# Reordering two ScalarE steps of the K/V phase and adding 72 matmuls to the first attention tile of a transformer layer on eight cores

## Chip, cores and metric

The kernel runs on the 8 cores of one Trainium2 chip. Every core works on two of the 16 sequences and exchanges nothing with the others. The metric is the device time of the slowest core in microseconds.

## What is computed

One post-norm transformer layer: linear attention (elu + 1 as feature map, 16 heads of 64), then an FFN with SiLU gate and integer weights, each with a residual and a layer norm.

```python
q = elu(x @ Wq.T) + 1; k = elu(x @ Wk.T) + 1; v = x @ Wv.T       # x: (16, 2048, 1024)
KV = einsum('bshd,bshe->bhde', k, v); k_sum = k.sum(axis=1)
out = einsum('bshd,bhde->bshe', q, KV) / (einsum('bshd,bhd->bsh', q, k_sum) + 1e-6)
x = layernorm(x + out @ Wo.T)
h = silu(x @ (w_gate/127).T) * (x @ (w_up/127).T)                # hidden 3072
x = layernorm(x + h @ (w_down/127).T)
```

## The kernel before

Each core takes its two sequences of 2048 tokens in turn. The order of instructions on each engine is the order in which the program text issues them; semaphores tie the engines together, and every DMA is issued on SyncE's one queue (SP).

**Phase 1** (`phase1`, once for a sequence) computes K, V and the sum of k^T v over 16 chunks of 128 tokens. Numbers u of chunks count from 0. For a chunk:
- PE: 16 matmuls of K (L552) into one pair of PSUM banks (`kps`), 16 of V (L568) into the other (`vps`). The pairs swap roles with each chunk: K of chunk u+1 writes the banks that held V of chunk u, and V of chunk u+1 those that held K of u. Then come 16 small matmuls k^T v of the chunk before (L486, `emit_kv`).
- DVE adds these into `kv_acc` (L504), takes min(K, 0) into `t1` (L585), and later writes `k_tm` = max(K, 0) + exp (L604).
- ACT takes the exponential `texp` of `t1` (L590) and copies V from PSUM to `v_tm` (L596). Ahead of them in a chunk it casts the next chunk's x to bf16 (L450). SP loads x two chunks ahead (L441) and transposes the cast x into `xT` (L459).

In the first sequence the same loop also converts weights (`drain_w_jobs`, four jobs a chunk): wq and wo in chunks 0 to 3, with a load, an ACT cast (L385) and a store each; w_down in chunks 4 to 9, with a load (L344) and a cast on DVE or GpSimd (L353) into `wd_buf`; then wk and wv are stored from `wpair` (L330). After phase 1 `load_pair` puts wq and wo where wk and wv were (L426).

**Phase 2** (`phase2`, once for a tile of 512 tokens, four to a sequence) computes Q (L816, 64 matmuls), multiplies by the summed KV in eight steps of 4 matmuls (L864, `emit_c1h`), each followed on DVE by three steps that free its banks, transposes the result by DMA (L925), projects it by wo (L941, `emit_c2`) and normalises (`ln_chunk`). Between these steps `pend_half` puts the down projection of the previous tile (L735, 48 matmuls for 128 tokens). In the very first tile there is no previous one: `pend` is None, and the first four calls of `pend_half` issue the loads of the first gate and up weights instead (`fill_jobs`, L1042), the last two nothing. `pre_pend` is true in the first tile of each sequence, `skip_a` in every tile.

**Phase 3** (`phase3`) computes gate (L1135) and up (L1148) in 24 blocks and h (L1167 on ACT, L1175 on DVE).

PE's matmuls in the places above are 128x512, except L864 (128x130) and L486 (128x65). The two operations that the change swaps, in their order before:

```python
t_exp = P.op("scalar", lambda e: e.activation(texp[:], t1[:], AF.Exp), waits=[t_min, ...])
t_v = P.op("scalar", lambda e: e.activation(v_tm[:, kr, :, 0:HD], vps[:]..., AF.Copy), waits=brd(vbk) + ...)
```

Of the kernel before, what the change touches and what calls it, by code (L numbers as in the profile page):

```python
# [10 lines left out]
AF = mybir.ActivationFunctionType  # L11
# [171 lines left out]
def build_program(n_seq=NSEQ, n_tiles=NTILE // NSEQ, stop_after=None):  # L183
# [17 lines left out]
    with contextlib.ExitStack() as ctx:  # L201
        E = ctx.enter_context
        wpair = E(nc.sbuf_tensor("wpair", [128, 2, NJ, D], BF16))
        wd_buf = E(nc.sbuf_tensor("wd_buf", [128, NM, D], BF16))
# [14 lines left out]
        t1 = E(nc.sbuf_tensor("t1", [128, D], BF16))  # L219
        texp = E(nc.sbuf_tensor("texp", [128, D], BF16))  # L220
# [10 lines left out]
        P = Prog(nc, ctx)  # L231
# [3 lines left out]
        def bw(keys):  # L235
            return [BK[k].begin_write() for k in keys]
# [4 lines left out]
        def bend(keys, tok):  # L241
            for k in keys:
                BK[k].end_write(tok)
# [8 lines left out]
        d_view = ps_c[:].rearrange("p (r e) -> p r e", r=2)  # L252
# [12 lines left out]
        tr_t1 = Track()  # L265
        tr_texp = Track()
# [9 lines left out]
        tr_wd = [Track() for _ in range(NM)]  # L276
# [8 lines left out]
        tok = P.op("vector", lambda v: v.memset(consts[:, 0:1], EPS_LN))  # L285
        tr_consts.add_write(tok)
        tok = P.op("vector", lambda v: v.memset(consts[:, 1:2], -0.5))
        tr_consts.add_write(tok)
        tok = P.op("vector", lambda v: v.memset(consts[:, 2:3], INV127))
        tr_consts.add_write(tok)  # L290
        for r in range(2):
            tok = P.op("vector", lambda v, r=r: v.memset(v_tm[:, r, :, HD:HD + 1], 1.0))
# [180 lines left out]
        def phase1(s, first, pre_x=False):  # L473
            NCH = SEQ // 128
            pend = {}
# [58 lines left out]
            for u in range(NCH):  # L534
                p1_cast(u + 1)
                tq = order[u] % CPT
                kr = u % 2
                kvr = u % 2
                if first:
                    drain_w_jobs(4)  # L540

                kps = ps_a if u % 2 == 0 else ps_b
                vps = ps_b if u % 2 == 0 else ps_a
                kbk = ("a0", "a1") if u % 2 == 0 else ("b0", "b1")
                vbk = ("b0", "b1") if u % 2 == 0 else ("a0", "a1")
                for j in range(NJ):
                    for hl in range(2):
                        last = (j == NJ - 1 and hl == 1)
                        tok = P.op(
                            "tensor",  # L550
                            lambda t, j=j, hl=hl, tq=tq, kps=kps:
                            t.matmul(kps[:, hl * 512:(hl + 1) * 512],  # L552
                                     xT[:, j, tq * 128:(tq + 1) * 128],
                                     wpair[:, 0, j, hl * 512:(hl + 1) * 512],
                                     start=(j == 0), stop=(j == NJ - 1)),
                            waits=[tr_xT[tq].reads(), tr_wp[0][j].reads()]
                                  + (bw(kbk) if (j == 0 and hl == 0) else []),
                            inc=last)
                bend(kbk, tok)
                p1_ld(u + 2)  # L560
                p1_tp(u + 1)
                for j in range(NJ):
                    for hl in range(2):
                        last = (j == NJ - 1 and hl == 1)
                        tok = P.op(
                            "tensor",
                            lambda t, j=j, hl=hl, tq=tq, vps=vps:
                            t.matmul(vps[:, hl * 512:(hl + 1) * 512],  # L568
                                     xT[:, j, tq * 128:(tq + 1) * 128],
                                     wpair[:, 1, j, hl * 512:(hl + 1) * 512],  # L570
                                     start=(j == 0), stop=(j == NJ - 1)),
                            waits=[tr_xT[tq].reads(), tr_wp[1][j].reads()]
                                  + (bw(vbk) if (j == 0 and hl == 0) else []),
                            inc=last)
                bend(vbk, tok)
                tr_xT[tq].add_reader(tok)
                for j in range(NJ):
                    tr_wp[0][j].add_reader(tok)
                    tr_wp[1][j].add_reader(tok)

                if u > 0:
                    emit_kv(u - 1)

                t_min = P.op("vector",
                             lambda v, kps=kps: v.tensor_scalar_min(t1[:], kps[:], 0.0),  # L585
                             waits=brd(kbk) + [tr_t1.begin_write()])
                bread(kbk, t_min)
                tr_t1.end_write(t_min)
                t_exp = P.op("scalar",
                             lambda e: e.activation(texp[:], t1[:], AF.Exp),  # L590
                             waits=[t_min, tr_texp.begin_write()])
                tr_t1.add_reader(t_exp)
                tr_texp.end_write(t_exp)
                t_v = P.op("scalar",
                           lambda e, kr=kr, vps=vps:
                           e.activation(v_tm[:, kr, :, 0:HD],  # L596
                                        vps[:].rearrange("p (h e) -> p h e", h=H),
                                        AF.Copy),
                           waits=brd(vbk) + [tr_vtm[kr].begin_write()])
                bread(vbk, t_v)  # L600
                tr_vtm[kr].add_write(t_v)
                t_k = P.op("vector",
                           lambda v, kr=kr, kps=kps:
                           v.scalar_tensor_tensor(k_tm[:, kr, :], kps[:], 0.0,  # L604
                                                  texp[:], ALU.max, ALU.add),
                           waits=[t_exp] + brd(kbk)
                                 + [tr_ktm[kr].begin_write()])
                bread(kbk, t_k)
                tr_texp.add_reader(t_k)
                tr_ktm[kr].end_write(t_k)  # L610
                pend[u] = (kr, kvr, t_k, t_v)

            emit_kv(NCH - 1)
            if first:
# [4 lines left out]
                      waits=[tr_kvbd.begin_write()])  # L619
            c0 = P.op("vector",  # L620
                      lambda v: v.tensor_copy(kvbd[0:64, :, 0:HD + 1],
                                              kv_acc[0:64, :, :]),
                      waits=[z0, tr_kvacc.reads()])
# [3 lines left out]
                      waits=[z0, tr_kvacc.reads()])  # L627
# [99 lines left out]
        def down_half(sc, hl):  # L727
            pr = sc % 2
            bank = ("c0", "c1", "c2", "c3")[pr * 2 + hl]
            for hm in range(NM):  # L730
                last = (hm == NM - 1)
                tok = P.op(
                    "tensor",
                    lambda t, hm=hm, hl=hl, sc=sc, pr=pr:
                    t.matmul(d_view[:, pr, hl * 512:(hl + 1) * 512],  # L735
                             h_fm[:, hm, sc * 128:(sc + 1) * 128],
                             wd_buf[:, hm, hl * 512:(hl + 1) * 512],
                             start=(hm == 0), stop=(hm == NM - 1)),
                    waits=[tr_h[hm].reads(), tr_wd[hm].reads()]
                          + (bw((bank,)) if hm == 0 else []),  # L740
                    inc=last)
            bend((bank,), tok)
            for hm in range(NM):
                tr_h[hm].add_reader(tok)
                tr_wd[hm].add_reader(tok)
            down_toks[(sc, hl)] = tok
# [33 lines left out]
        def phase2(s, g, stop2=None, skip_a=False, pend=None, slot3=3,  # L780
# [6 lines left out]
            def px(step):  # L787
# [13 lines left out]
                elif step == 5:  # L801
                    load_x_fin(nxt[2], 2)
                    load_x_fin(nxt[3], 3)

            if pre_pend and pend is not None:
                down_half(0, 0)
                down_half(0, 1)
            q_toks = {}
            for i in range(NJ):
                abk = "a0" if i % 2 == 0 else "a1"  # L810
                for j in range(NJ):
                    last = (j == NJ - 1)
                    tok = P.op(
                        "tensor",
                        lambda t, i=i, j=j:
                        t.matmul(ps_a[:, (i % 2) * 512:(i % 2 + 1) * 512],  # L816
                                 wpair[:, 0, j, i * 128:(i + 1) * 128],
                                 xT[:, j, :], start=(j == 0), stop=(j == NJ - 1)),
                        waits=[tt.reads() for tt in tr_xT] + [tr_wp[0][j].reads()]
                              + (bw((abk,)) if j == 0 else []),  # L820
                        inc=last)
# [3 lines left out]
                for tt in tr_xT:  # L825
                    tt.add_reader(tok)
                t_min = P.op("vector",
                             lambda v, i=i:
# [13 lines left out]
                           lambda v, i=i:  # L842
# [135 lines left out]
            def pend_half(sc, hl):  # L978
                if pend is not None:
                    down_half(sc, hl)  # L980
                elif fill_jobs:
                    fill_jobs.pop(0)()

            def pend_fin(sc):
                if pend is not None:
# [303 lines left out]
```

How the kernel before makes its waits and increments, by code:

```python
        def closure(eng, fn=fn, real_waits=real_waits, tok=tok, sem=sem):  # L128
            for s, v in real_waits:
                eng.wait_ge(s, v)
            inst = fn(eng)
            if tok is not None:
                inst.then_inc(sem, 1)
# [15 lines left out]
        def closure(e, fn=fn, real_waits=real_waits, sem=sem):  # L149
            for s, v in real_waits:
                e.wait_ge(s, v)
            fn(e).then_inc(sem, 16)
# [7 lines left out]
        def closure(eng, real_waits=real_waits):  # L160
            for s, v in real_waits:
                eng.wait_ge(s, v)
```

## Time and profile before

| what | us |
|---|---|
| median of the two timed runs | 1977.47 |
| the two timed runs | 1959.79 and 1995.15 |
| the profiled execution | 1951.59 |
| its span, first to last instruction of core 1 | 1950.1 |
| phase 1 of the first sequence, first K matmul to last kv matmul | 19 to 267 |
| the first tile's Q to its first gate matmul | 270 to 354 |
| phase 1 of the second sequence | 991 to 1205 |

The profile is of the slowest core of one execution. The span leaves out what lies before the first and behind the last instruction. Engines: PE is the matmul engine, DVE the vector engine, ACT the scalar engine, SPq the queue on which SyncE issues DMAs. In a row of the timeline the first number is the start, the second the time that the row covers; in brackets stands how long the engine was idle ahead of it and what ended that.

### The profile page before, as it was taken

What the parts mean: (1) busy time and instruction counts of PE and PEld (TensorE: products, weight loads), DVE (VectorE), ACT (ScalarE), POOL (GpSimd) and SP (SyncE); (2) the same over time, 40 slices, a digit from 0 to 9 for tenths busy, and PEclk for the clock granted to TensorE, in tenths of its full rate; (3) what the DMA queues carried; (4) which work ended last, traced back from release to release, by engine and by line L of the source; (5) the groups of instructions that cost most, each with busy time, mean ns of one, the idle gap of its engine ahead of it and who ended that gap; (6) DMA issues with size and microseconds to landing.
All of it is one profiled execution on the core that took longest, in us unless ns stands there. A gap on an engine that the chain in (4) does not pass through costs nothing.

```text
span 1950.1 us, 23065 instructions; the slowest of 8 cores (1931.0 to 1950.1 us)
## 1 busy us (share of the span) xinstructions
PE 1602.9 (82%) x7424; PEld 697.3 (36%) x7424; DVE 520.4 (27%) x979; ACT 541.8 (28%) x801; POOL 42.3 (2%) x44
## 2 busy tenths in 40 slices
PE   2666664778999899997986677889899989989998
PEld 0222221333444344443432223334344434434443
DVE  1132232123321332332222222421331232133211
ACT  2421211212342252233112221341243225223312
POOL 0010001121000000000000000000000000000000
PEclk9888886899999999998997888989999999999999
DMA  7987227795444145336522222245235515522431
GB/s 221 268 252 251 44 87 205 216 314 194 105 129 155 55 109 168 103 91 195 152 81 65 49 54 92 65 120 154 81 112 141 150 53 131 153 76 62 130 112 44
DMA packets 213236, 255.28 MB, mean 131 GB/s; under 512 B 136320, under 2 KB 136320, under 8 KB 212096
## 3 DMA queue, kind: packets, MB, share of 16 engines
q1 hardware_dynamic: 213120, 253.81, 45.0%
q8 instruction: 64, 1.05, 0.2%
q14 instruction: 52, 0.43, 0.1%
HBM read 184.55 MB, written 37.75 MB: 114 GB/s over the span
## 4 chain that ended last, share of the span: by engine, by line
PE 68%; DMA 10%; DVE 8%; ACT 6%; issue 5%; SPq 1%; POOL 1%; DVEq 0%; ACTq 0%; POOLq 0%
PE ps_c L735 18%; PE ps_a L1135 15%; PE ps_b L1148 15%; PE ps_b L941 5%; PE ps_a L552 4%; PE ps_b L552 4%; PE ps_a L568 2%; PE ps_b L568 2%; DVE t L829 2%; ACT texp L836 2%; DVE t L585 2%; PE ps_a L816 2%; DVE q_fm L843 2%; DMA scr_wu<-wgu 1%; ACT v_tm L596 1%
## 5 line engine op out<-in xcount | busy, mean ns | idle before, releaser
L1135 PE MATMUL ps_a<-ln1T,wgu 128*128 128x512 bf16 x1536 | 369.0, 384 | 26.2 <-DMA ln1T<-ln_bf 9.4
L1148 PE MATMUL ps_b<-ln1T,wgu 128*128 128x512 bf16 x1536 | 368.5, 383 | 19.2 <-DVE h_fm L1175 19.2
L735 PE MATMUL ps_c<-wd_buf,h_fm 128*128 128x512 bf16 x1536 | 354.3, 390 | 0.0
L1167 ACT ACTIVATE silu_b<-ps_a,consts 128x512 bf16<-128x512 f32 x192 | 131.4, 688 | 521.1 <-PE ps_a L1135 461.4
L1175 DVE SCALAR_TENSOR_TENSOR h_fm<-ps_b,silu_b 128x512 bf16<-128x512 f32 x192 | 131.9, 691 | 489.1 <-PE ps_b L1148 454.9
L1135 PEld LDWEIGHTS ps_a<-ln1T,wgu 128*128 128x128 bf16 x1536 | 151.2, 99 | 214.8 <-issue 39.9
L1148 PEld LDWEIGHTS ps_b<-ln1T,wgu 128*128 128x128 bf16 x1536 | 150.6, 99 | 207.2 <-issue 31.9
L735 PEld LDWEIGHTS ps_c<-wd_buf,h_fm 128*128 128x128 bf16 x1536 | 153.2, 101 | 185.7 <-issue 19.3
L552 PE MATMUL ps_a<-wpair,xT 128*128 128x512 bf16 x256 | 88.3, 515 | 98.7 <-ACT v_tm L596 57.7
L941 PE MATMUL ps_b<-wpair,attnT 128*128 128x512 bf16 x512 | 135.0, 424 | 30.5 <-DVE res L965 14.2
L816 PE MATMUL ps_a<-xT,wpair 128*128 128x512 bf16 x512 | 126.8, 398 | 30.9 <-DVE q_fm L843 27.2
L639 ACT ACTIVATE texp<-res 128x1024 bf16<-128x1024 f32 x64 | 67.3, 1051 | 297.3 <-DVE res L758 233.9
L552 PE MATMUL ps_b<-wpair,xT 128*128 128x512 bf16 x256 | 86.0, 511 | 73.3 <-ACT v_tm L596 65.7
L590 ACT ACTIVATE texp<-t 128x1024 bf16<-128x1024 bf16 x32 | 33.7, 1055 | 293.2 <-DVE t L585 292.8
L941 PEld LDWEIGHTS ps_b<-wpair,attnT 128*128 128x128 bf16 x512 | 53.3, 107 | 102.4 <-issue 60.5
L504 DVE TENSOR_TENSOR kv_acc<-kv_acc,ps_c 128x520 f32<-128x520 f32 x30 | 20.9, 697 | 251.9 <-PE ps_c L486 251.9
L816 PEld LDWEIGHTS ps_a<-xT,wpair 128*128 128x128 bf16 x512 | 48.7, 101 | 107.4 <-issue 62.0
L552 PEld LDWEIGHTS ps_a<-wpair,xT 128*128 128x128 bf16 x256 | 29.9, 123 | 150.7 <-issue 140.8
L552 PEld LDWEIGHTS ps_b<-wpair,xT 128*128 128x128 bf16 x256 | 30.8, 125 | 123.1 <-issue 112.9
L836 ACT ACTIVATE texp<-t 128x512 bf16<-128x512 bf16 x64 | 40.3, 629 | 120.4 <-DVE t L829 120.4
L864 PE MATMUL ps_a<-kvbd,q_fm 128*128 128x130 bf16 x256 | 29.4, 238 | 49.4 <-DVE attn_bf L906 30.8
L843 DVE SCALAR_TENSOR_TENSOR q_fm<-ps_a,texp 128x512 bf16<-128x512 f32 x64 | 44.3, 692 | 64.3 <-ACT texp L836 64.3
(61 smaller groups left out, 879.1 us busy)
## 6 DMA issues: line engine op xcount, KB each, us to landing
wgu<-scr_wg SPq DMA_DIRECT2D x168, 256.0 KB, 2.6
wgu<-scr_wu SPq DMA_DIRECT2D x168, 256.0 KB, 2.6
x_f<-x SPq DMA_DIRECT2D x56, 512.0 KB, 4.4
out<-outb SPq DMA_DIRECT2D x32, 512.0 KB, 2.7
outb<-wgi SPq DMA_DIRECT2D x14, 512.0 KB, 6.4
outb<-wui SPq DMA_DIRECT2D x14, 512.0 KB, 7.2
outb<-wdi SPq DMA_DIRECT2D x12, 512.0 KB, 5.0
wgu<-wdi SPq DMA_DIRECT2D x12, 512.0 KB, 6.5
```

The costliest lines, as they stand in the source:

```text
L552: t.matmul(kps[:, hl * 512:(hl + 1) * 512], xT[:, j, tq * 128:(tq + 1) * 128], wpair[:, 0, j, hl * 512:(hl + 1) * 512], start=(j == 0), st ...
L568: t.matmul(vps[:, hl * 512:(hl + 1) * 512], xT[:, j, tq * 128:(tq + 1) * 128], wpair[:, 1, j, hl * 512:(hl + 1) * 512], start=(j == 0), st ...
L639: e.activation(texp[:], res[:, rr, :], AF.Square, accum_out=stats[:, sl, 1:2]),
L735: t.matmul(d_view[:, pr, hl * 512:(hl + 1) * 512], h_fm[:, hm, sc * 128:(sc + 1) * 128], wd_buf[:, hm, hl * 512:(hl + 1) * 512], start=(hm ...
L816: t.matmul(ps_a[:, (i % 2) * 512:(i % 2 + 1) * 512], wpair[:, 0, j, i * 128:(i + 1) * 128], xT[:, j, :], start=(j == 0), stop=(j == NJ - 1)),
L836: lambda e: e.activation(texp[:, 0:TILE], t1[:, 0:TILE], AF.Exp),
L843: v.scalar_tensor_tensor(q_fm[:, i, :], ps_a[:, (i % 2) * 512:(i % 2 + 1) * 512], 0.0, texp[:, 0:TILE], ALU.max, ALU.add),
L941: t.matmul(ps_b[:, hl * 512:(hl + 1) * 512], attnT[:, tc, e_, :], wpair[:, 1, e_, hl * 512:(hl + 1) * 512], start=(e_ == 0), stop=(e_ == N ...
L1135: t.matmul(ps_a[:, (m % 2) * 512:(m % 2 + 1) * 512], wgu[:, 0, r, j * 128:(j + 1) * 128], ln1T[:, j, :], start=(j == 0), stop=(j == NJ - 1)),
L1148: t.matmul(ps_b[:, (m % 2) * 512:(m % 2 + 1) * 512], wgu[:, 1, r, j * 128:(j + 1) * 128], ln1T[:, j, :], start=(j == 0), stop=(j == NJ - 1)),
L1167: e.activation(silu_b[:, m % 2, :], ps_a[:, (m % 2) * 512:(m % 2 + 1) * 512], AF.Silu, scale=consts[:, 2:3]),
L1175: v.scalar_tensor_tensor(h_fm[:, m, :], ps_b[:, (m % 2) * 512:(m % 2 + 1) * 512], INV127, silu_b[:, m % 2, :], ALU.mult, ALU.mult),
```

## The change

Two edits. In phase 1 the ACT copy of V is issued ahead of the exponential, in all 32 chunks. In phase 2 a function `warm_mms(n)` issues n matmuls of 128x512 whose result, in PSUM bank c0, nobody reads (`wd_buf` times `wd_buf`). It is called with 24 ahead of Q, and with 8 in every call of `pend_half` without a pending tile. Both occur in the first tile of the first sequence alone: 24 + 6 x 8 = 72 matmuls. The branch with `not skip_a` is never taken.

```diff
@@ phase1
-                t_exp = P.op("scalar",
-                             lambda e: e.activation(texp[:], t1[:], AF.Exp),
-                             waits=[t_min, tr_texp.begin_write()])
-                tr_t1.add_reader(t_exp)
-                tr_texp.end_write(t_exp)
                 t_v = P.op("scalar",
...
                 tr_vtm[kr].add_write(t_v)
+                t_exp = P.op("scalar",
+                             lambda e: e.activation(texp[:], t1[:], AF.Exp),
+                             waits=[t_min, tr_texp.begin_write()])
+                tr_t1.add_reader(t_exp)
+                tr_texp.end_write(t_exp)
@@ phase2
+            def warm_mms(n):
+                for i in range(n):
+                    last = (i == n - 1)
+                    tok = P.op(
+                        "tensor",
+                        lambda t:
+                        t.matmul(d_view[:, 0, 0:512],
+                                 wd_buf[:, 0, 0:128],
+                                 wd_buf[:, 1, 0:512],
+                                 start=True, stop=True),
+                        waits=[tr_wd[0].reads(), tr_wd[1].reads()]
+                              + (bw(("c0",)) if i == 0 else []),
+                        inc=last)
+                bend(("c0",), tok)
+                tr_wd[0].add_reader(tok)
+                tr_wd[1].add_reader(tok)
+
             if pre_pend and pend is not None:
                 down_half(0, 0)
                 down_half(0, 1)
+            elif pre_pend and pend is None and not skip_a:
+                pass
+            elif pre_pend:
+                warm_mms(24)
@@ pend_half
-                elif fill_jobs:
-                    fill_jobs.pop(0)()
+                else:
+                    if fill_jobs:
+                        fill_jobs.pop(0)()
+                    warm_mms(8)
```

On ACT, in chunk 1 of the first sequence, with its last weight cast ahead and the cast of x of the next chunk behind:

```order
 L385 ACTIVATE h_fm<-res 128x1024 [waits sem_scalar,dsl_wf0,dsl_scw3]
-L590 ACTIVATE texp<-t 128x1024 [waits sem_vector,sem_scalar]
-L596 ACTIVATE v_tm<-ps_a 128x16x64 [waits sem_tensor]
+L591 ACTIVATE v_tm<-ps_a 128x16x64 [waits sem_tensor]
+L598 ACTIVATE texp<-t 128x1024 [waits sem_vector,sem_scalar]
 L450 ACTIVATE x_bf<-x_f 128x1024 [waits dsl_x1]
```

The copy of V, which waits for the matmuls of V alone, now stands ahead of the exponential, which waits for DVE. All else on ACT keeps its place.

On PE, before, from the last kv matmuls of the first sequence over the first tile's attention to phase 3:

```order
L486 MATMUL ps_c<-v_tm,k_tm 64x65 x32
L816 MATMUL ps_a<-xT,wpair 128x512 x64
L864 MATMUL ps_a<-kvbd,q_fm 128x130 x16
L941 MATMUL ps_b<-wpair,attnT 128x512 x16
L864 MATMUL ps_a<-kvbd,q_fm 128x130 x8
L941 MATMUL ps_b<-wpair,attnT 128x512 x16
L864 MATMUL ps_a<-kvbd,q_fm 128x130 x8
L941 MATMUL ps_b<-wpair,attnT 128x512 x32
```

And in the changed kernel, at the start of the same stretch (L811 are the added matmuls, L837 is Q, L885 the product with KV, L962 the projection by wo):

```order
L486 MATMUL ps_c<-v_tm,k_tm 64x65 x32
L811 MATMUL ps_c<-wd_buf 128x512 x24
L837 MATMUL ps_a<-xT,wpair 128x512 x64
L885 MATMUL ps_a<-kvbd,q_fm 128x130 x8
L811 MATMUL ps_c<-wd_buf 128x512 x8
L885 MATMUL ps_a<-kvbd,q_fm 128x130 x4
L811 MATMUL ps_c<-wd_buf 128x512 x8
L885 MATMUL ps_a<-kvbd,q_fm 128x130 x4
L962 MATMUL ps_b<-wpair,attnT 128x512 x16
```

And at its end, where phase 3 begins (L1158):

```order
L885 MATMUL ps_a<-kvbd,q_fm 128x130 x8
L962 MATMUL ps_b<-wpair,attnT 128x512 x32
L811 MATMUL ps_c<-wd_buf 128x512 x16
L1158 MATMUL ps_a<-ln1T,wgu 128x512 x8
```

Added are 24 matmuls ahead of Q, 8 ahead of four of the steps with KV, and 16 behind the last projection. Nothing else moved on PE.

## Rows read from the trace of the kernel before

**Rows 1.** The page's first line, the slowest of eight cores.

```profile
span 1950.1 us, 23065 instructions; the slowest of 8 cores (1931.0 to 1950.1 us)
```

**Rows 2.** K matmuls (L552): idle us until each releaser, times.

```profile
  ACT v_tm L596: 123.4, 28
...
  DMA xT<-x_bf: 12.2, 2
```

**Rows 3.** Timeline of one chunk, sequence 2: start, us, engine, line, instruction.

```profile
1017.92 3.62 PE L568 MATMUL ps_b<-wpair,xT 128*128 128x512 bf16 x16
...
1021.47 0.45 PE L486 MATMUL ps_c<-v_tm,k_tm 128*64 128x65 bf16 x16
1022.09 0.69 DVE L504 TENSOR_TENSOR kv_acc<-kv_acc,ps_c 128x520 f32<-128x520 f32 x1 [10.15 <-PE ps_c L486]
1022.70 1.22 DVE L585 TENSOR_SCALAR t<-ps_a 128x1024 bf16<-128x1024 f32 x1
1024.07 1.06 ACT L590 ACTIVATE texp<-t 128x1024 bf16<-128x1024 bf16 x1 [12.54 <-DVE t L585]
1025.03 1.01 ACT L596 ACTIVATE v_tm<-ps_b 128x1024 bf16<-128x1024 f32 x1
1025.23 1.22 DVE L604 SCALAR_TENSOR_TENSOR k_tm<-ps_a,texp 128x1024 bf16<-128x1024 f32 x1 [1.31 <-ACT texp L590]
1025.93 1.05 ACT L450 ACTIVATE x_bf<-x_f 128x1024 bf16<-128x1024 f32 x1
...
1026.29 5.88 PE L552 MATMUL ps_b<-wpair,xT 128*128 128x512 bf16 x16 [4.38 <-ACT v_tm L596]
```

**Rows 4.** Timeline of PE, phase 1 of the second sequence.

```profile
1000.03 3.61 PE L552 MATMUL ps_b<-wpair,xT 128*128 128x512 bf16 x16 [1.48 <-ACT v_tm L596]
1003.48 3.62 PE L568 MATMUL ps_a<-wpair,xT 128*128 128x512 bf16 x16
...
1190.40 5.74 PE L552 MATMUL ps_b<-wpair,xT 128*128 128x512 bf16 x16 [4.38 <-ACT v_tm L596]
```

**Rows 5.** Timeline of PE, phase 1 of the first sequence.

```profile
102.21 5.30 PE L552 MATMUL ps_a<-wpair,xT 128*128 128x512 bf16 x16 [4.84 <-ACT v_tm L596]
...
115.72 5.30 PE L552 MATMUL ps_b<-wpair,xT 128*128 128x512 bf16 x16 [4.38 <-ACT v_tm L596]
...
169.76 5.77 PE L552 MATMUL ps_b<-wpair,xT 128*128 128x512 bf16 x16 [4.38 <-ACT v_tm L596]
...
197.24 5.30 PE L552 MATMUL ps_b<-wpair,xT 128*128 128x512 bf16 x16 [4.38 <-ACT v_tm L596]
...
252.12 5.30 PE L552 MATMUL ps_b<-wpair,xT 128*128 128x512 bf16 x16 [4.47 <-ACT v_tm L596]
```

**Rows 6.** Windows: stretch, length, busy us of each engine, granted clock, DMA share, GB/s.

```profile
57.22:102.21 44.99, 28.34 (x144) 11.60 (x145) 9.00 (x9) 20.99 (x22) 0.00 (x0) 0.84 0.99 265
115.72:169.76 54.04, 36.52 (x193) 15.29 (x194) 17.88 (x21) 11.66 (x13) 9.81 (x9) 0.85 0.68 218
169.76:197.24 27.48, 18.72 (x96) 7.70 (x97) 7.30 (x9) 5.82 (x7) 0.00 (x0) 0.86 0.81 239
1026.29:1190.40 164.11, 111.53 (x576) 46.16 (x577) 36.67 (x37) 34.70 (x36) 0.00 (x0) 0.83 0.22 52
276.01:289.80 13.79, 11.32 (x49) 4.27 (x49) 8.03 (x13) 3.78 (x6) 0.00 (x0) 1.00 0.00 1
298.72:351.00 52.28, 23.50 (x80) 9.08 (x80) 12.80 (x35) 15.70 (x27) 8.32 (x8) 0.66 0.72 191
```

**Rows 7.** DMA issues: queue, kind, count, median us to landing.

```profile
xT<-x_bf SPq DMA_TRANSPOSE x56, 3.2
```

**Rows 8.** Timeline of PE, end of phase 1 to phase 3, first sequence.

```profile
266.04 0.47 PE L486 MATMUL ps_c<-v_tm,k_tm 128*64 128x65 bf16 x16 [4.79 <-DVE k_tm L604]
...
270.13 5.09 PE L816 MATMUL ps_a<-xT,wpair 128*128 128x512 bf16 x16 [3.62 <-DMA wpair<-scr_wq]
...
315.74 6.16 PE L941 MATMUL ps_b<-wpair,attnT 128*128 128x512 bf16 x16 [5.36 <-DMA attnT<-attn_bf]
...
353.77 3.57 PE L1135 MATMUL ps_a<-ln1T,wgu 128*128 128x512 bf16 x8 [9.37 <-DMA ln1T<-ln_bf]
```

## Prediction

> **What bounds the kernel now.** I read the page first, then the waits of the K matmuls, then one chunk of phase 1 in order of time, and last the windows by stage. The span is 1950.1 us on core 1, and the cores lie within 1% of each other [rows 1]. The one large wait that this change touches is in phase 1, the K and V projections of 32 chunks of 128 tokens: the K matmuls (L552) sat idle for 123.4 us in 28 waits until ACT's copy of V (L596), about 4.4 us each, and for 12.2 us until a transpose of x [rows 2].
>
> One chunk in order of time shows why the wait is that long [rows 3]. V's matmuls start at 1017.92 and end at 1021.54, and the small kv matmuls end at 1021.92. Then a chain runs: DVE adds kv into kv_acc (0.69), DVE takes the minimum of K (1.22), ACT the exponential (1.06), and only then ACT copies V out of ps_b (1.01). V had been complete since 1021.54, but ACT works its queue in order and the exponential stands ahead. PE needs ps_b for the next K and starts at 1026.29, after 4.38 us of idleness. The second half of the price is in that same row: the 16 K matmuls then take 5.88 us, while 16 V matmuls take 3.62. The granted clock over this part of phase 1 is 0.83 [rows 6]: it falls to its lower level, 1.2 GHz, in each stall and comes back to 2.4 GHz in the course of K. A stall of 1.48 us did not do that: the K at 1000.03 took 3.61 us after it and V started 3.45 us after K, which is 0.216 us a matmul [rows 4]. Eight matmuls at the low level took 3.57 us, about 0.43 each [rows 8].
>
> **The swap on ACT, second sequence.** V's copy goes ahead of the exponential. It then waits for V's matmuls alone. The row at 1000.03 shows what that gives: behind the first chunk of the sequence, which has no kv step ahead of its exponential, V's copy alone was missing, and K came after 1.48 us of idleness [rows 4]. So K can start at V's end + 1.48 and, at full clock, end its stream 3.45 later, at + 4.93. The exponential loses nothing: its input is ready 2.4 us after V's end (1023.92 less 1021.54), the copy is over by about 1.2, and k_tm ends as now, at 1025.23 + 1.22 = 1026.45, which is 4.91 behind V's end [rows 3]. That is the wait that is late next: V of the next chunk writes the bank that k_tm reads, so it starts at + 4.91 + 0.2 = + 5.1, and with 3.62 for V itself the period becomes 8.7 us. PE is then idle for about 1.0 us ahead of K and 0.2 ahead of V. The Q stage has a comparable pattern, PE busy 11.32 of 13.79 us in short stalls, with a granted clock of 1.00 [rows 6], so I take the clock as held. The K starts of 1000.03 and 1190.40 are 14 periods apart [rows 4], 13.60 us each. 14 x (13.60 - 8.7) = 68.6 us. The last K goes from 5.74 to 3.62: 2.1 us.
>
> Queued behind the exponential on ACT is the cast of x (L450), and behind it on SP's queue the transpose of x, which lands in 3.2 us at the median [rows 7]. The cast now follows k_tm's input as before, so it ends about 4.8 us behind V's end and the transpose lands at about 8.3; the K that reads it starts at 8.7 + 1.5 = 10.2. That is hidden with 2 us to spare. DMA was busy for 0.22 of this stretch, 3 us a chunk of the 13.6 [rows 6], so it has room here.
>
> **The swap, first sequence.** The same chunks run beside the conversion of the other weights, and the DMA share tells how much can be gained [rows 6].
> - Chunks 1 to 3 (57.22 to 102.21): DMA is at 0.99. ACT also carries four weight casts a chunk ahead of both operations, each waiting for its DMA. I take 1.0 us in all, the copy that no longer stands behind the exponential at the end.
> - Chunk 4 (102.21 to 115.72, 13.51 us [rows 5]): K starts cold, then the short stall. A stream takes 0.17 less than its row says, since the next begins under its end (3.62 and 3.45): 5.13 + 3.45 + 1.48 = 10.1, a gain of 3.4.
> - Chunks 5 to 8 (115.72 to 169.76): share 0.68 of 54.04 is 36.7 us of DMA, 9.2 a chunk, more than 8.7. I take 9.5, since loads, stores and transposes share one queue and don't pack fully: 54.0 - 38.0 = 16.0. Ends: 8.7 (gain 19.2) and no gain at all, if each load group must land before the next is issued.
> - Chunks 9 and 10 (169.76 to 197.24), with the stores of wk and wv, 2 MB each: 0.81 x 27.48 = 22.3 us of DMA is the floor: 5.2. Ends 10.1 and 0.
> - Chunks 11 to 14 (197.24 to 252.12), nothing beside them: 54.88 - 4 x 8.7 = 20.1, and the last K 1.7.
> Sum of the first sequence 47.4, of the second 70.7.
>
> **The 24 matmuls ahead of Q.** They enter after the kv matmuls, which end at 266.04 + 0.47 = 266.5 [rows 8], where PE now waits until 270.13 for wq. The kv matmuls had a 4.79 us stall ahead, so the clock is low: 24 x 0.216 + 1.7 for the ramp (as in K, 5.30 against 3.62 [rows 5, 4]) = 6.9, until 273.4. Q starts 3.3 later than the weights allow but without its own ramp (5.09 against 3.62): net 1.8 us lost. Ends: 0.1 (24 at 0.216) and 5.2 (24 at 0.43).
>
> **The six groups of 8.** They stand between the attention steps of the first tile. Each costs 1.7 us of PE at full clock and 3.4 at the low one. There PE is busy for 23.50 of 52.28 us with DMA at 0.72 [rows 6], and the second projection by wo waited 5.36 us for the DMA of attnT [rows 8]. That transpose stands on SP's queue behind the loads of gate and up weights, which don't hang on PE. Four groups lie where PE waits for DVE or DMA, two (16 matmuls) in the 9.37 us in front of the first gate matmul at 353.77 [rows 8]; they end too early to warm it. I take 0. Ends: 48 x 0.43 = 20.6 lost, or 7.5 gained, if three projections of 16 run as V does (3.62 in place of 6.16).
>
> **A rule weighed.** The rows put the ramp at 29 K groups of about 1.7 us, 49 us or 2.5% of the span. The Trainium skill, page "TensorE: Matmul & The Clock Gate", Part 1, holds that the ramp penalty is under 1% of a typical kernel's span. By that rule the clock could give back at most 19.5 us in place of about 49, and the sum would come out some 30 us smaller. The trace disagrees, since the cold start returns with every chunk.
>
> **The sum.** 47.4 + 70.7 - 1.8 = 116.3 us. The profiled execution took 1951.59 us, 1.5 more than its span, which gives 1835.3. The two timed runs are 8.2 and 43.6 above that execution, their median 25.9; I go by the lower and predict 1843.
>
> **Rivals.**
> 1. The two short stalls together still drop the clock at each K. Then a period is 1.48 + 5.13 + 3.46 = 10.1: 14 x 3.5 = 49 in the second sequence, 38 in the first (1.0 + 3.4 + 13.6 + 5.2 + 14.5), less 1.8: 85, or 1875 us. For it: 4.4 us of stall do it every time. Against: the K behind 1.48 us, and the Q stage.
> 2. SP's one queue binds where weights are converted: chunks 5 to 10 keep their time. The sum loses 21.2: 95 and 1865 us. For it: share 0.68 to 0.81, and K waited for xT twice. Against: the queue is idle for a third of that time.
> 3. The copy was not what PE waited for (the profile names the latest event only), and nothing is gained. Then only the added matmuls count, 2 to 20 us: about 1970. Against: the 28 waits of equal length.
> 4. Slower: phase 1 is split into stalls too short for a pause and too frequent for the clock, which stays at 1.2 GHz through K and V. The period is then 6.9 + 6.9 + 1.5 = 15.3 against 13.6; over 25 chunks 42 us, and 72 added matmuls at 0.43 are 31: up to 73 slower, 2033 us. It decides as soon as V too runs at 0.43. Against: the same rows as in 1; each V behind a slow K took 3.62 us.
>
> **Chances.** The forecast 0.74, rival 1 0.09, rival 2 0.12, rival 3 0.03, rival 4 0.02. The low end takes DMA at its best (8) and the gain in the projections (7.5) with a base at the profiled time: 1835 - 15 = 1820, and 5 for small things: 1815. The high end takes rivals 1 and 2 and 20 us for a base at the median: 1892. A measurement tells 2%, some 39 us, from no change; rivals 1 and 2 are beyond it as well, so faster 0.95, same 0.03, slower 0.02.
>
> **What would show it.** Right: in the second sequence K starts 8.7 us apart, K's 16 matmuls take 3.6, the granted clock there is near 1.00, the idle time of L552 until V's copy is near 1 us a chunk, and a new wait of V (L568) for k_tm appears. The added matmuls stand from about 219 us (266 less 47) for about 7 us, and Q right behind. Wrong: K of 5 us after the short stall (rival 1), K waiting for xT in chunks 5 to 10 (rival 2), K still 4 us behind V (rival 3), V of 6.8 us (rival 4), or more than 89 us from Q's start to the first gate matmul, which are 84 now.

## The result and the profile after

The changed kernel took 1844.88 us in the median of 9 runs (1840.81 to 1852.92). The kernel before, run beside it, took 1952.15 in the median of 8. The ratio is 0.945, with a 95% interval of 0.9428 to 0.9473: 107 us less. Some executions on all eight cores were disturbed, with longer times on the same kernel; the medians and ratios below leave them out, and where that left too few for an interval, the text gives the lowest time. The forecast was 1843 us and faster, so the total fits. It is so close by luck in part: two errors cancel, told below.

The page of the changed kernel, its first line and the engines' busy time, answers to [rows 1]:

```profile
span 1848.0 us, 23214 instructions; the slowest of 8 cores (1826.4 to 1848.0 us)
...
PE 1571.8 (85%) x7496; PEld 690.3 (37%) x7496; DVE 520.2 (28%) x979; ACT 544.9 (29%) x801; POOL 42.6 (2%) x44
```

PE is busy for 31 us less (1602.9 before) although 72 matmuls were added: K's 16 matmuls take 3.61 us in most chunks now, where they took 5.30 and more. The waits of K (L552), against [rows 2]:

```profile
  DMA xT<-x_bf: 28.5, 7
  ACT v_tm L591: 20.8, 20
  ACT texp L598: 15.1, 3
```

Of 123.4 us behind V's copy 20.8 are left, 1.04 each. The wait for transposes of x grew from 12.2 to 28.5 us; a third entry names the exponential, three waits ahead of chunks 3 to 5, of which more below.

One chunk of the second sequence in order of time, which answers to [rows 3]:

```profile
997.04 3.61 PE L568 MATMUL ps_b<-wpair,xT 128*128 128x512 bf16 x16
...
1000.58 0.45 PE L486 MATMUL ps_c<-v_tm,k_tm 128*64 128x65 bf16 x16
1000.75 1.03 ACT L591 ACTIVATE v_tm<-ps_b 128x1024 bf16<-128x1024 f32 x1 [4.24 <-PE ps_b L568]
1001.21 0.70 DVE L504 TENSOR_TENSOR kv_acc<-kv_acc,ps_c 128x520 f32<-128x520 f32 x1 [4.31 <-PE ps_c L486]
1001.82 1.22 DVE L585 TENSOR_SCALAR t<-ps_a 128x1024 bf16<-128x1024 f32 x1
...
1002.03 3.61 PE L552 MATMUL ps_b<-wpair,xT 128*128 128x512 bf16 x16 [1.00 <-ACT v_tm L591]
1003.48 1.06 ACT L598 ACTIVATE texp<-t 128x1024 bf16<-128x1024 bf16 x1 [1.70 <-DVE t L585]
...
1004.64 1.23 DVE L604 SCALAR_TENSOR_TENSOR k_tm<-ps_a,texp 128x1024 bf16<-128x1024 f32 x1 [1.60 <-ACT texp L598]
...
1006.01 3.61 PE L568 MATMUL ps_a<-wpair,xT 128*128 128x512 bf16 x16 [0.37 <-DVE k_tm L604]
```

V's matmuls end at 1000.65, ACT copies V at 1000.75 instead of behind the exponential, and K starts at 1002.03, 1.00 us after PE's last kv matmul. K takes 3.61 us. The new wait is in the last row: V of the next chunk stands until DVE's k_tm step has read its banks. Here it is 0.37 us; in most chunks V starts 3.69 us behind K, where a free stream takes 3.45.

Three windows, the second sequence and chunks 5 to 8 and 9 to 10 of the first, against [rows 6] (columns as there):

```profile
984.71:1089.38 104.67, 91.21 (x577) 39.79 (x578) 36.94 (x37) 36.35 (x36) 0.00 (x0) 1.00 0.40 81
112.57:150.20 37.63, 31.45 (x193) 14.01 (x193) 16.48 (x20) 10.96 (x11) 8.88 (x8) 0.95 1.11 314
150.20:175.56 25.36, 15.20 (x96) 6.62 (x97) 9.55 (x10) 8.11 (x8) 2.30 (x2) 0.86 1.07 331
```

The granted clock of the second sequence went from 0.83 to 1.00. In the first sequence the DMA share passed 1. A share above 1 can only arise where the times of packets overlap, so 1 is not a full engine and no ceiling.

To place the gain I compared the same start times on PE on all eight cores, before and after. Each row is the mean length of a stage over the cores in one execution.

| stage | before | after | forecast change | measured change |
|---|---|---|---|---|
| sequence 1, chunks 1 to 3 | 43.1 | 43.5 | -1.0 | +0.4 |
| chunk 4 | 13.8 | 10.6 | -3.4 | -3.2 |
| chunks 5 to 8 | 54.6 | 37.2 | -16.0 | -17.4 |
| chunks 9 and 10 | 27.2 | 26.8 | -5.2 | -0.4 |
| chunks 11 to 14 | 55.0 | 36.7 | -20.1 | -18.3 |
| last K to the last kv | 14.4 | 13.1 | -1.7 | -1.3 |
| last kv to Q | 3.4 | 6.8 | +3.3 | +3.4 |
| Q to the first gate matmul | 82.2 | 80.2 | -1.5 | -2.0 |
| from there to the second tile's Q | 111.0 | 112.9 | 0 | +1.9 |
| to sequence 2 | 523.1 | 525.2 | 0 | +2.1 |
| phase 1 of sequence 2 | 213.4 | 143.2 | -70.7 | -70.2 |
| the rest | 744.9 | 745.8 | 0 | +0.9 |

### The profile page after: what moved, and what is told of

The parts are those of the page before. It is cut to its first block, busy times and chain, and to the rows that moved or that the text cites. A ratio compares the mean times of both kernels' runs of the same rounds, so it can differ in the third digit from the quotient of the medians.

```text
span 1848.0 us, 23214 instructions; the slowest of 8 cores (1826.4 to 1848.0 us)
## 1 busy us (share of the span) xinstructions
PE 1571.8 (85%) x7496; PEld 690.3 (37%) x7496; DVE 520.2 (28%) x979; ACT 544.9 (29%) x801; POOL 42.6 (2%) x44
## 4 chain that ended last, share of the span: by engine, by line
PE 67%; DMA 12%; DVE 7%; ACT 6%; issue 4%; SPq 2%; POOL 1%; DVEq 0%; ACTq 0%; POOLq 0%
PE ps_c L735 18%; PE ps_a L1158 16%; PE ps_b L1171 15%; PE ps_b L962 5%; PE ps_b L552 3%; PE ps_a L552 3%; PE ps_a L568 3%; DMA outb<-wui 3%; PE ps_b L568 2%; DVE t L850 2%; ACT texp L857 2%; DMA xT<-x_bf 2%; DVE q_fm L864 2%; PE ps_a L837 2%; DMA attnT<-wui 1%
## 5 line engine op out<-in xcount | busy, mean ns | idle before, releaser
L1158 PE MATMUL ps_a<-ln1T,wgu 128*128 128x512 bf16 x1536 | 367.0, 382 | 23.2 <-DMA wgu<-scr_wg 8.6
L1158 PEld LDWEIGHTS ps_a<-ln1T,wgu 128*128 128x128 bf16 x1536 | 150.4, 98 | 209.7 <-issue 33.3
L962 PE MATMUL ps_b<-wpair,attnT 128*128 128x512 bf16 x512 | 131.9, 417 | 33.4 <-DMA attnT<-attn_bf 16.3
L837 PE MATMUL ps_a<-xT,wpair 128*128 128x512 bf16 x512 | 125.3, 394 | 27.4 <-DVE q_fm L864 27.4
L552 PE MATMUL ps_a<-wpair,xT 128*128 128x512 bf16 x256 | 67.0, 415 | 59.2 <-ACT wpair L415 35.4
L552 PE MATMUL ps_b<-wpair,xT 128*128 128x512 bf16 x256 | 63.0, 403 | 40.5 <-DMA xT<-x_bf 19.5
L962 PEld LDWEIGHTS ps_b<-wpair,attnT 128*128 128x128 bf16 x512 | 52.4, 105 | 102.8 <-issue 59.1
L837 PEld LDWEIGHTS ps_a<-xT,wpair 128*128 128x128 bf16 x512 | 48.6, 100 | 102.8 <-issue 56.3
L885 PE MATMUL ps_a<-kvbd,q_fm 128*128 128x130 bf16 x256 | 28.7, 234 | 43.3 <-DVE attn_bf L927 24.8
L758 DVE SCALAR_TENSOR_TENSOR res<-ps_c,ln_bf 128x1024 f32<-128x1024 f32 x32 | 39.0, 1219 | 82.8 <-PE ps_c L735 79.9
L552 PEld LDWEIGHTS ps_a<-wpair,xT 128*128 128x128 bf16 x256 | 24.8, 102 | 95.1 <-issue 72.8
L568 PE MATMUL ps_b<-wpair,xT 128*128 128x512 bf16 x256 | 59.1, 384 | 0.6
L450 ACT ACTIVATE x_bf<-x_f 128x1024 bf16<-128x1024 f32 x56 | 57.5, 1041 | 4.8 <-DMA x_f<-x 4.8
```

Of the source, the lines that this page charges most:

```text
L552: t.matmul(kps[:, hl * 512:(hl + 1) * 512], xT[:, j, tq * 128:(tq + 1) * 128], wpair[:, 0, j, hl * 512:(hl + 1) * 512], start=(j == 0), st ...
L568: t.matmul(vps[:, hl * 512:(hl + 1) * 512], xT[:, j, tq * 128:(tq + 1) * 128], wpair[:, 1, j, hl * 512:(hl + 1) * 512], start=(j == 0), st ...
L837: t.matmul(ps_a[:, (i % 2) * 512:(i % 2 + 1) * 512], wpair[:, 0, j, i * 128:(i + 1) * 128], xT[:, j, :], start=(j == 0), stop=(j == NJ - 1)),
L962: t.matmul(ps_b[:, hl * 512:(hl + 1) * 512], attnT[:, tc, e_, :], wpair[:, 1, e_, hl * 512:(hl + 1) * 512], start=(e_ == 0), stop=(e_ == N ...
L1158: t.matmul(ps_a[:, (m % 2) * 512:(m % 2 + 1) * 512], wgu[:, 0, r, j * 128:(j + 1) * 128], ln1T[:, j, :], start=(j == 0), stop=(j == NJ - 1)),
```

## Experiments

Theory: three engines share one chain. The kv addition stands ahead of K's minimum on DVE and waits for PE, the exponential waits for that minimum, and V's copy stood behind the exponential; the stall that this makes also lowers the clock. The rivals are named with each run.

**The swap without the added matmuls.**

```diff
-            elif pre_pend and pend is None and not skip_a:
-                pass
-            elif pre_pend:
-                warm_mms(24)
...
-                else:
-                    if fill_jobs:
-                        fill_jobs.pop(0)()
-                    warm_mms(8)
+                elif fill_jobs:
+                    fill_jobs.pop(0)()
```

> The change without its 72 added matmuls. Theory (the swap carries the whole gain, the added matmuls cost a little ahead of Q): 1843 us, within 3 us of the changed kernel and if anything below it; periods of 8.7 us in the second sequence; Q starts about 3.4 us after the last kv matmul instead of 6.7, but its first 16 matmuls take 5.1 us. Rival (the added matmuls warm the attention stage and pay): 5 to 10 us slower than the changed kernel, near 1852.

Lowest time 1836.82 us, without an interval; the same kernel stands below once more. The profile has what the expectation said of stages: the second sequence takes 143.2 us as with the change, Q starts 3.2 us behind the last kv matmul instead of 6.8, and Q to the first gate matmul is 82.2 instead of 80.2 (means over the cores; the 82.2 is what the kernel before has too). PE on core 0, from the last kv matmuls on:

```profile
215.37 0.65 PE L486 MATMUL ps_c<-v_tm,k_tm 128*64 128x65 bf16 x16 [4.79 <-DVE k_tm L604]
218.37 5.02 PE L833 MATMUL ps_a<-xT,wpair 128*128 128x512 bf16 x16 [2.34 <-DMA wpair<-scr_wq]
...
246.84 6.13 PE L958 MATMUL ps_b<-wpair,attnT 128*128 128x512 bf16 x16
...
301.66 3.57 PE L1152 MATMUL ps_a<-ln1T,wgu 128*128 128x512 bf16 x8 [9.46 <-DMA ln1T<-ln_bf]
```

Q pays its ramp (5.02 us for 16 matmuls) and the first projection by wo runs slowly (6.13).

**The added matmuls alone.**

```diff
+                t_exp = P.op("scalar",
...
                 t_v = P.op("scalar",
...
-                t_exp = P.op("scalar",
```

> The 72 added matmuls alone, with the ACT order of before. Theory: no gain, 1950 to 1957 us (1952 plus 0 to 5), phase 1 as before with periods of 13.6 us. Rival (they pay): 1942 to 1947.

1949.95 us, ratio 0.9989 (0.9964 to 1.0013): no difference. Phase 1 of the second sequence is 213.1 us as before, last kv to Q 6.8, Q to gate 80.4. So the swap carries the gain.

In the changed kernel the same stage reads as follows on PE of core 5, against [rows 8]:

```profile
224.14 0.66 PE L486 MATMUL ps_c<-v_tm,k_tm 128*64 128x65 bf16 x16 [4.79 <-DVE k_tm L604]
224.72 7.95 PE L811 MATMUL ps_c<-wd_buf 128*128 128x512 bf16 x24
232.51 3.62 PE L837 MATMUL ps_a<-xT,wpair 128*128 128x512 bf16 x16
...
260.19 3.61 PE L962 MATMUL ps_b<-wpair,attnT 128*128 128x512 bf16 x16
...
276.94 5.71 PE L962 MATMUL ps_b<-wpair,attnT 128*128 128x512 bf16 x16 [7.37 <-DMA attnT<-attn_bf]
...
314.74 3.57 PE L1158 MATMUL ps_a<-ln1T,wgu 128*128 128x512 bf16 x8 [5.61 <-DMA ln1T<-ln_bf]
```

The 24 matmuls take 7.95 us, and Q starts behind them at the high clock (3.62). The first projection runs in 3.61, with two groups of 8 between the steps ahead of it (6.13 without them, above). The second waits 7.37 us for the DMA of attnT and is slow all the same (5.71). So is the first gate block (3.57), 5.61 us behind the last group. From Q to the first gate matmul it takes 2.0 us less in the mean; 1.6 of these are Q's own 64 matmuls (19.4 to 17.8), so the six groups give next to nothing. I read that as the waits for transposes taking back what PE gains; no run took the two apart.

**The addition moved on DVE, the ACT order as before.**

```diff
     def emit_kv(u):
...
-        acc = P.op("vector", ...)      # kv_acc += kv of chunk u
+        accq.append((u, kvr, cbk, tok))
...
     pend[u] = (kr, kvr, t_k, t_v)
+    emit_acc()                         # the same addition, behind k_tm
```

> The kernel before with one other edit: DVE's addition into kv_acc is issued behind k_tm, so that the minimum of K no longer stands behind it; exponential and V copy keep the old order on ACT. Theory (what made the exponential late was the DVE queue: the addition waits for the kv matmuls, which stand behind V): the exponential is ready before V ends, K starts 1.5 us behind V's end and V directly behind K, period 8.4 us; total 1835 us, 8 less than the swap alone. Rival (the order on ACT is the cause, and only the swap removes it): 13.6 us periods and 1952.

1825.26 us, ratio 0.9336 (0.9277 to 0.9394). The rival is out: with the exponential still ahead of V's copy on ACT, the stall is gone. A chunk of the second sequence on core 0, in order of time:

```profile
1004.05 3.61 PE L558 MATMUL ps_b<-wpair,xT 128*128 128x512 bf16 x16 [1.00 <-ACT v_tm L602]
...
1007.50 3.62 PE L574 MATMUL ps_a<-wpair,xT 128*128 128x512 bf16 x16
1007.84 1.22 DVE L591 TENSOR_SCALAR t<-ps_b 128x1024 bf16<-128x1024 f32 x1 [3.92 <-PE ps_b L558]
1009.21 1.06 ACT L596 ACTIVATE texp<-t 128x1024 bf16<-128x1024 bf16 x1 [4.47 <-DVE t L591]
1010.37 1.23 DVE L610 SCALAR_TENSOR_TENSOR k_tm<-ps_b,texp 128x1024 bf16<-128x1024 f32 x1 [1.31 <-ACT texp L596]
...
1011.21 1.03 ACT L602 ACTIVATE v_tm<-ps_a 128x1024 bf16<-128x1024 f32 x1 [0.94 <-PE ps_a L574]
...
1012.49 3.61 PE L558 MATMUL ps_a<-wpair,xT 128*128 128x512 bf16 x16 [1.00 <-ACT v_tm L602]
```

K's minimum (1007.84) starts under V's matmuls and no longer behind the addition, the exponential (1009.21) ends before V does, and ACT is idle when V ends, so the copy starts at once (1011.21). K starts after 1.00 us, V directly behind K, and the period is 8.44 us (1012.49 less 1004.05) against 8.7 with the swap. The ACT order mattered only because DVE's order made the exponential late. The edit also shortens the end of phase 1, from the last K to the last kv matmul, from 13.1 us with the swap to 8.8 in each sequence, as the last k_tm is early. In the first sequence PE then waits 7.1 us for wq instead of 3.2, so only the second gains by it. The expectation had left that out; it is some 4 of the 10 us by which the total came out lower than it said.

**Matmuls in the stall, all else as before.**

```diff
                 if u > 0:
                     emit_kv(u - 1)
+                    fbk = ("c0", "c1") if kvr == 0 else ("c2", "c3")
+                    for i in range(14):
+                        tok = P.op("tensor", ...)   # wpair x wpair, 128x512, into d_view[:, kvr, 0:512]
+                    bend(fbk, tok)
```

> The kernel before with 14 matmuls of 128x512 (3.0 us, result unread) in each phase 1 chunk behind the kv matmuls, in the stall of 4.4 us; nothing else changed. It separates the two parts of the gain. Theory (a part of about 1.7 us a chunk is the clock that falls in the stall): K takes 3.6 instead of 5.3 us with the stall as long as before, period 11.8, gain 14 x 1.8 in the second and about 11 x 1.6 in the first sequence, 1910 us. Rival (K is slow behind a stall for another cause, for example its PSUM banks): K stays at 5.3 and the total at 1952.

1905.09 us, ratio 0.9752 (0.9702 to 0.9802), 2 to 3% less. The order and length of the chain are untouched, and yet some 47 us go. Core 1, sequence 2 (L588 are the filling matmuls):

```profile
1015.06 3.62 PE L568 MATMUL ps_b<-wpair,xT 128*128 128x512 bf16 x16
...
1018.99 3.19 PE L588 MATMUL ps_c<-wpair 128*128 128x512 bf16 x14
...
1023.43 3.61 PE L552 MATMUL ps_b<-wpair,xT 128*128 128x512 bf16 x16 [1.25 <-ACT v_tm L611]
...
1026.88 3.62 PE L568 MATMUL ps_a<-wpair,xT 128*128 128x512 bf16 x16
```

From V's end (1018.68) to K is 4.75 us, as before. Only K changed, from 5.3 us and more to 3.61, and the granted clock of this stretch is 1.00, where it was 0.83. This is the clock's part of the stall: 11.82 us a period (186.7 against 213.4 for the sequence) with the wait kept. The swap takes both parts: of its 4.9 us a period 1.8 are clock and 3.1 are the wait.

**The changed kernel, beside the next three.**

> The changed kernel itself, beside the next three. Both theories: 1845 us.

1842.4 us, ratio 0.9431 (0.936 to 0.9503).

**The swap without the added matmuls, again.**

> The swap without the 72 matmuls once more, since the first time left the interval open. Theory (the 24 matmuls delay Q by 3.3 us and give 2.5 back in the attention stage): between 0 and 5 us faster than the changed kernel. Rival (they pay): 3 us or more slower than it.

Ratio 0.9421 (0.9348 to 0.9493), lowest 1834.91 against 1837.24 for the changed kernel. The totals can't be told apart. By stage means, last kv to the second tile's Q takes 193.8 and 195.1 us in the two executions without the added matmuls, and 199.9 and 198.7 with them, while the cores of one execution scatter by 5 us (standard deviation). That they pay is not borne out. One stage tells more: from the first gate matmul to the second tile's Q the three executions with the added matmuls take 112.3 to 113.2 us in the mean, the eight without them 107.9 to 111.0. So the added matmuls go with some 3 us there, for a cause that no run shows, and a cost of a few us is likely, but too small for the totals to show.

**The large stores cut.**

```diff
-            w_jobs.append(("pair_st", mat, si, 0))
+            for j in range(NJ):
+                w_jobs.append(("pair_st", mat, si, j))
...
-                    drain_w_jobs(4)
+                    if u < 10:
+                        drain_w_jobs(4)
+                    else:
+                        if u == 10:
+                            flush_w_stores()
+                        drain_w_jobs(3)
```

> The swap without the 72 matmuls, and the two stores of 2 MB (wk, wv) cut into 16 of 256 KB, three a chunk from chunk 10 on. Theory (chunks 9 and 10 gained nothing in the changed kernel because K waited for a transpose of x queued behind those 4 MB): these two chunks fall from 25 to 27 us to about 19, no wait of 9 us for xT; total 6 us below the swap alone, about 1836. Rival (DMA volume binds there wherever the stores stand): the time appears again in chunks 11 to 15 and the total stays.

Ratio 0.9374 (0.9308 to 0.944), lowest 1827.14. The interval overlaps that of the swap alone, so the difference is read from the stages: chunks 9 and 10 take 19.3 us against 25.5 in the same kernel with whole stores, and chunks 11 to 14 35.7 against 36.5, together 7 us. The same bytes are stored by the end of the phase, and the time doesn't appear again, so the rival is out. PE on core 1, the K groups of chunks 10 to 12:

```profile
153.65 5.02 PE L555 MATMUL ps_a<-wpair,xT 128*128 128x512 bf16 x16 [2.44 <-DMA xT<-x_bf]
...
163.82 3.61 PE L555 MATMUL ps_b<-wpair,xT 128*128 128x512 bf16 x16 [1.33 <-DMA xT<-x_bf]
...
173.40 5.30 PE L555 MATMUL ps_a<-wpair,xT 128*128 128x512 bf16 x16 [2.13 <-DMA xT<-x_bf]
```

The waits for xT are 1.3 to 2.4 us here, and on no core more than 3.6, where the changed kernel has one of 9.0 to 10.9 ahead of chunk 11 on each.

**The addition moved, V copied by halves, the stores cut.**

```diff
-                for j in range(NJ):
-                    for hl in range(2):
+                for hl in range(2):
+                    for j in range(NJ):
...
+                for hh in range(2):                        # copy half hh as soon as its 8 matmuls end
+                    t_v = P.op("scalar", ...)
```

> The late addition on DVE (old ACT order), the K and V matmuls of a chunk ordered by output half so that V is copied in two halves, and the stores spread. Theory (with the chain of k_tm off the path, only V's copy of 1.0 us is exposed, and halves hide it): period 7.4 us in the second sequence against 8.4, which is 14 us, some 5 in the first, where DMA binds, and 6 of the stores: 1800 us. Rival (something behind PE binds at 8.4, such as the cast and transpose of x): 1819.

1799.42 us, ratio 0.9225 (0.9182 to 0.9268), better than the kernel before and the changed one. A chunk of sequence 2 on core 0, and the window of that phase:

```profile
1003.29 0.58 ACT L606 ACTIVATE v_tm<-ps_b 128x512 bf16<-128x512 f32 x1
...
1004.21 0.45 PE L485 MATMUL ps_c<-v_tm,k_tm 128*64 128x65 bf16 x16
1004.43 0.60 ACT L606 ACTIVATE v_tm<-ps_b 128x512 bf16<-128x512 f32 x1 [0.56 <-PE ps_b L577]
...
1004.59 3.63 PE L561 MATMUL ps_b<-wpair,xT 128*128 128x512 bf16 x16
...
1008.05 3.62 PE L577 MATMUL ps_a<-wpair,xT 128*128 128x512 bf16 x16
...
1011.60 0.45 PE L485 MATMUL ps_c<-v_tm,k_tm 128*64 128x65 bf16 x16
...
1011.98 3.62 PE L561 MATMUL ps_a<-wpair,xT 128*128 128x512 bf16 x16
```

```profile
960.00:1080.00 120.00, 117.70 (x750) 53.35 (x747) 50.44 (x54) 42.81 (x57) 0.00 (x0) 1.00 0.37 106
```

The first half of V is copied under the second half's matmuls, the second half (1004.43) under K's first, and K follows the kv matmuls directly: 7.39 us from K to K, PE busy for 117.70 of 120 us. Phase 1 of the sequence takes 120.0 us.

**The halves with the stores whole.**

> The late addition on DVE and the copy of V by halves, with the two stores of 2 MB left whole. It tells how much of the last run came from which edit. Theory (periods of 7.4 us from the halves, about 6 us from the stores): 1804 to 1808, chunks 9 and 10 together 24 to 27 us, second sequence as in the run before. Rival (with PE faster still, the large stores cost more, since less PE time lies over them): 1812 or more.

Lowest 1803.69 us, no interval. Chunks 9 and 10 are back at 25.8 us (19.1 with the stores cut), but chunks 11 to 14 take 31.5 against 33.5, so 4.7 us net are the stores' and the rest of the step from 1825 is the halves', 15.8 of it in the second sequence (135.8 to 120.0).

## Why the prediction was right, and where it was not

**The mechanism.** V's copy was held by the exponential, that by the steps ahead of it on DVE, and the stall cost a wait and a ramp (K's first matmuls at the low clock): right at each step. The late addition (1825 us with the old ACT order) shows the chain, the filled stall (1905) the clock's part, some 47 us against the 49 that the prediction read from the rows. The period was forecast at 8.7 us and is 8.72 (104.67 for the 12 periods of the first window); the sum for the second sequence was 70.7 and is 70.2. The wait that would be late next was named: V for k_tm, 0.37 us where it shows.

**Rivals 1 and 4** (the clock falls all the same) are out in the second sequence, at a granted clock of 1.00. **Rival 3** (nothing gained) is out by the result itself.

**Rival 2 and the step that failed.** It said that chunks 5 to 10 keep their time because SP's one queue binds. In chunks 5 to 8 they don't: 37.2 us against my 38.0, at a DMA share above 1. For chunks 9 and 10 the rival was right and my term wrong: I took "0.81 x 27.48 = 22.3 us of DMA" as the floor and a gain of 5.2 us, and 0.4 was measured. Chunk 9 takes 9.0 us in the mean and chunk 10 17.8. The floor was no floor, as share times length is not a fixed amount: chunks 5 to 8 moved the same 11.8 MB before and after (218 GB/s over 54.04 us, 314 over 37.63), for 36.7 us by the share before and 41.8 after. What holds chunk 10 up is 4 MB that stand ahead of one transpose in the queue. The rows of SP and ACT in the changed kernel, and of PE:

```profile
154.77 0.61 SPq L330 DMA_DIRECT2D scr_wk<-wpair  x1
155.43 1.38 SPq L330 DMA_DIRECT2D scr_wv<-wpair  x1
156.92 3.58 SPq L392 DMA_DIRECT2D scr_wo<-h_fm  x3
...
160.59 0.54 SPq L441 DMA_DIRECT2D x_f<-x  x1
...
162.16 7.16 SPq L459 DMA_TRANSPOSE xT<-x_bf  x1
...
174.56 1.06 ACT L450 ACTIVATE x_bf<-x_f 128x1024 bf16<-128x1024 f32 x1 [4.79 <-DMA x_f<-x]
```

```profile
112.57 3.61 PE L552 MATMUL ps_b<-wpair,xT 128*128 128x512 bf16 x16 [3.32 <-ACT texp L598]
...
140.07 5.30 PE L552 MATMUL ps_a<-wpair,xT 128*128 128x512 bf16 x16 [2.02 <-DMA xT<-x_bf]
...
175.56 5.21 PE L552 MATMUL ps_b<-wpair,xT 128*128 128x512 bf16 x16 [9.01 <-DMA xT<-x_bf]
```

Issue to landing, first of the two stores (L330), then of the four transposes from 150 to 190 us (L459):

```profile
DMA to landing us min/median/max: 11.1/13.3/15.5
```

```profile
DMA to landing us min/median/max: 3.1/4.7/13.3
```

The stores of wk and wv (2 MB each) are issued at 154.77 and 155.43, and the transpose for the next K at 162.16 behind them. It reached SBUF 13.3 us later, where the median is 3.2. The transfers landed in the order of their issue: the two stores at 165.8 and 171.0, the load of x at 174.4, the transpose at 175.4. K waited 9.01 us for it, at 175.56. Before, that transpose was issued 12.7 us behind the first store instead of 7.4, landed in 7.3 us, and K came later still. The faster loop uncovered it, and the run with the stores cut takes 6.2 us out of it (25.5 to 19.3). That run shortens what stands ahead of each transpose and thins the traffic at once (331 GB/s in this window of the changed kernel); whole stores behind the transpose, which would part the two, were not run.

The K at 112.57 waited 3.32 us, and the profile names the exponential, as it does for the two K ahead of it. In the code K does not wait for it. It waits for the transposes of its x, and these landed 9.5, 8.0 and 11.4 us behind their issue at 76.61, 91.95 and 101.07, within 0.2 us of the three starts. I read all three as waits for what stood ahead in the queue, at a DMA share near 1; no run took them apart.

**Small terms.** Chunks 1 to 3 gained nothing where I gave 1.0; chunks 11 to 14 took 9.2 us each and not 8.7, nearly all of it in chunk 11 (10.6), whose K ran slowly behind the wait of 9 us (5.21), while the three behind it took 8.4 to 9.0. The added matmuls cost 1.4 us up to the first gate matmul against 1.8 forecast. Of the four us behind it (+1.9 and +2.1 in the table), which no term had, the first goes with the added matmuls, as told above, and its cause is open; the second is not there in the changed kernel's other profiled execution (524.2 against 523.1 before). Core 5 is the slowest by 12 us against the mean of the spans, and 6 of these are in that first stage (119 against 113).

**The base.** The sum was 116.3 us off a profiled execution of 1951.59, and I then added 8.2 us for the lower of two timed runs. With more runs the kernel before had a median of 1952.15, so hardly anything should have been added, and the measured gain was 107, 9 less than the sum. About 5 of these 9 are chunks 9 and 10. The two errors cancel in 1843 against 1845; the range would have held without that.

## What to carry to other kernels

When an engine waits for a copy that stands behind another operation on its queue, follow that other operation back as well: here the cause was one engine further, and moving the DVE addition alone gave a ratio of 0.9336 where the swap alone gave 0.9421. Their intervals overlap, but phase 1 of the second sequence is 7.4 us shorter with it and the mean span of the cores 11 to 12 us. Price a stall on PE with the ramp behind it, here 4.4 us and 1.7 us. And where a loop gets faster, look for the transfer that stands behind a large one on a shared queue: a mean DMA share does not show it.

## Not expected of the hardware

The length of a stall alone did not tell what the clock would do. In the rows above K ran in 3.61 us at the high clock behind 3.32 us of idleness (112.57), and took 5.30, at first at the low one, behind 2.02 (140.07) and behind 2.13 (173.40 in the run with the stores cut). In the steady loop with 1.00 us a chunk the granted clock was 1.00 over 104.67 us.

Transposes of 128x1024 that land in 3.2 us at the median took 11.4 and 13.3 us with 2 MB and more of plain transfers still under way that were issued ahead of them on the same queue.
